# Mixing q and k per batch: z's high and low halves stacked on the partitions

## The reference

```python
W = weights[condition]                       # 64 x 64 for each batch
h = einsum('bct,bcd->bdt', x, W)             # mix the channels
qkv = einsum('bsc,cf->bsf', h, Wqkv) + bqkv  # 768 columns: q 256, k 256, v 256
attn = softmax(q @ k.T / sqrt(256))
x = x + (attn @ v) @ Wo + bo
```

## Time and profile before

| what | value |
|---|---|
| median of three runs | 2296.03 us |
| the profiled execution, its own time | 2296.87 us |
| its span (first to last instruction) | 2295.2 us |
| busy share of the span | PE 98%, weight loads 76%, DVE 54%, ACT 42% |
| granted TensorE clock, mean | 0.996 of full speed |
| chain that ended last | PE 95%, DMA 2%, DVE 1% |

### The profile page before, as it was taken

The page is one execution under the profiler, slowest core; times in us unless marked ns, Lnnn a source line. Parts: engine busy times, 40 slices in busy tenths (PEclk is TensorE's granted clock), DMA queues, the critical chain, the costliest instruction groups (busy, mean ns, idle before and its releaser), DMA issues.

```text
span 2295.2 us, 73807 instructions
## 1 busy us (share of the span) xinstructions
PE 2251.0 (98%) x28506; PEld 1753.5 (76%) x28506; DVE 1238.0 (54%) x3438; ACT 953.9 (42%) x2461; POOL 61.6 (3%) x128
## 2 busy tenths in 40 slices
PE   7999999999999879999999999999999999999998
PEld 4777777777777578887878787878787878787876
DVE  7777777777777753444344434443444344434443
ACT  5776777667776642222222222222222222222221
POOL 4000000000000000000000000000000000000000
PEclk9999999999999999999999999999999999999999
DMA  7668777677677742131123132113215132331303
GB/s 286 250 256 303 266 275 286 259 279 278 247 278 261 282 162 112 39 130 57 53 97 130 57 128 95 57 57 129 94 57 201 41 111 72 115 112 39 130 20 111
DMA packets 108960, 356.46 MB, mean 155 GB/s; under 512 B 27600, under 2 KB 28752, under 8 KB 79184
## 3 DMA queue, kind: packets, MB, share of 16 engines
q1 hardware_dynamic: 97584, 279.84, 33.7%
q0 software_dynamic: 10112, 72.36, 8.5%
q10 hardware_dynamic: 1056, 1.05, 0.1%
HBM read 218.99 MB, written 134.22 MB: 154 GB/s over the span
## 4 chain that ended last, share of the span: by engine, by line
PE 95%; DMA 2%; DVE 1%; issue 1%; SPq 0%; ACT 0%; POOL 0%; DVEq 0%; ACTq 0%; POOLq 0%
PE bank L1168 21%; PE bank L1299 19%; PE bank L1270 19%; PE bank L1272 10%; PE bank L1301 10%; PE bank L1125 4%; PE bank L1126 4%; PE bank L1127 4%; PE bank L1281 1%; PE bank L1308 1%; PE bank L1309 1%; DMA stage<-w_in 1%; PE bank L1283 1%; DMA x<-xr 1%; DVE wf L874 0%
## 5 line engine op out<-in xcount | busy, mean ns | idle before, releaser
L1270 PE MATMUL bank<-xs,w 128*128 128x128 f16 x8192 | 627.9, 220 | 9.4 <-DVE xs L881 9.4
L1168 PE MATMUL bank<-w,xs 128*128 128x384 f16 x3072 | 552.9, 327 | 4.4 <-DVE w L894 4.4
L1270 PEld LDWEIGHTS bank<-xs,w 128*128 128x128 f16 x8192 | 480.9, 98 | 11.3 <-issue 9.9
L1299 PE MATMUL bank<-y,wf 128*128 128x512 f16 x2048 | 483.8, 379 | 0.8 <-DVE xr L924 0.8
L763 ACT ACTIVATE zh<-bank 128x256 f32<-128x256 f32 x256 | 97.7, 382 | 779.7 <-PE bank L1272 776.9
L1168 PEld LDWEIGHTS bank<-w,xs 128*128 128x128 f16 x3072 | 290.5, 98 | 164.8 <-DVE w L894 2.6
L1272 PE MATMUL bank<-xs,w 128*128 128x64 f16 x8192 | 407.3, 193 | 0.0
L920 DVE SCALAR_TENSOR_TENSOR xr<-bank,xr 128x256 f32 (+1 forms) x256 | 108.8, 425 | 432.5 <-PE bank L1309 387.5
L1299 PEld LDWEIGHTS bank<-y,wf 128*128 128x128 f16 x2048 | 197.0, 98 | 186.5 <-DVE xr L924 1.1
L1272 PEld LDWEIGHTS bank<-xs,w 128*128 128x128 f16 x8192 | 337.3, 98 | 0.0
L1301 PE MATMUL bank<-y,wf 128*128 128x256 f16 x2048 | 265.3, 273 | 0.0
(11 more groups left out here) (158 smaller groups left out, 2087.1 us busy)
## 6 DMA issues: line engine op xcount, KB each, us to landing
stage<-w_in SPq DMA_DIRECT2D x68, 1024.0 KB, 8.9
w<-ws POOLq DMA_DIRECT2D x68, 1024.0 KB, 6.6
ws<-wf SPq DMA_DIRECT2D x64, 1024.0 KB, 6.9
out<-xr SPq DMA_DIRECT2D x128, 256.0 KB, 2.3
xr<-x_in SPq DMA_DIRECT2D x31, 1024.0 KB, 8.0
x<-xr SPq DMA_DIRECT2D x31, 1024.0 KB, 4.4
xr<-x SPq DMA_DIRECT2D x124, 256.0 KB, 3.5
wcf<-wc_in SPq DMA_DIRECT2D x128, 32.0 KB, 4.5
```

Source lines behind the costliest of these rows:

```text
L1168: e = mm(zps[q % 2][h][:, 0:384], lhs, rhs[:, k, h * 384:(h + 1) * 384], start=(k == 0 and lhs is a and rhs is wq_h), stop=(k == K - 1 and ...
L1270: mm(both, hi[:, k, c], x_k, start=(k == 0), stop=False)
L1299: mm(fps[m % 2][:, :], wf_h[:, k, c], yhl[:, u, k, :], start=(k == 0), stop=False)
```

## The change

The high and low half of one batch's z are stacked on the partitions of one tile, `zs`: for batch b, z's high half stays on that batch's 64 partitions and its low half is written on the other 64. The q and k columns of z now go into one PSUM bank (512 columns) and the v columns into another (256). The mixing matrix of each batch is loaded twice, on both halves of the partitions, so that one matmul with 128 rows sums high x matrix and low x matrix. A block is then two matmuls (`wch`, `wcl`) of 64 columns for each batch: 16 of 64 columns where there were 12 of 128. The v columns keep the old scheme in tiles of their own, `zvh` and `zvl`. `z_hi` and `z_lo` become three instructions each: two of 64 partitions x 512 columns and one of 128 x 256, each with its own signal.

```diff
+        zs = zs_flat[:, :].rearrange("p (r b n) -> p r b n", r=2, b=2)
+        zvh = sb("zvh", [P, 2, DH], F16)
+        zvl = sb("zvl", [P, 2, DH], F16)
...
+        ZCOLS = ((0, 2 * DH), (2 * DH, 3 * DH))
...
                     sp.dma_start(dst, src).then_inc(s_wc[n], 16)
+                    again = wcf[(1 - b) * S:(2 - b) * S, n, b * S:(b + 1) * S]
+                    sp.dma_start(again, wc_in[bass.ds(e, 1), :, 0, :].rearrange("a c d -> (a c) d")
+                                 ).then_inc(s_wc[n], 16)
...
             def z_hi(i, q):
                 wait(act, s_z, i, 4, q + 1)
-                for h in range(2):
-                    e = nc.scalar.activation(zh[:, q % 2, h * 384:(h + 1) * 384], zps[q % 2][h][:, 0:384], Copy,
-                                             scale=SZ / (SX * SW))
-                e.then_inc(s_zh, 1)
+                for b in range(2):
+                    at = slice(b * S, (b + 1) * S)
+                    nc.scalar.activation(zs[at, q % 2, b, :], zps[q % 2][0][at, :], Copy,
+                                         scale=SZ / (SX * SW)).then_inc(s_zh, 1)
+                nc.scalar.activation(zvh[:, q % 2, :], zps[q % 2][1][:, 0:DH], Copy,
+                                     scale=SZ / (SX * SW)).then_inc(s_zh, 1)
...
             def z_lo(i, q):
+                for b in range(2):
+                    wait(dve, s_zh, i, 12, 3 * q + b + 1)
+                    at, other = slice(b * S, (b + 1) * S), slice((1 - b) * S, (2 - b) * S)
+                    v.scalar_tensor_tensor(out=zs[other, q % 2, b, :], in0=zps[q % 2][0][at, :],
+                                           scalar=SZ / (SX * SW), in1=zs[at, q % 2, b, :], op0=ALU.mult,
+                                           op1=ALU.subtract).then_inc(s_zl, 1)
+                wait(dve, s_zh, i, 12, 3 * q + 3)
+                v.scalar_tensor_tensor(out=zvl[:, q % 2, :], in0=zps[q % 2][1][:, 0:DH],
...
-                        for h in range(2):
-                            e = mm(zps[q % 2][h][:, 0:384], lhs, rhs[:, k, h * 384:(h + 1) * 384],
+                        for h, (lo, hi) in enumerate(ZCOLS):
+                            e = mm(zps[q % 2][h][:, 0:hi - lo], lhs, rhs[:, k, lo:hi],
...
-                wait(pe, s_zl, i, 4, q + 1)
                 wait(pe, s_wcl, i, 4, q + 1)
-                for c in range(4):
-                    d = slice(c * P, (c + 1) * P)
-                    e = three(qkps[:, d], [(zh[:, r, d], zl[:, r, d], wch[:, r, 0:P], wcl[:, r, 0:P])])
+                for b in range(2):
+                    wait(pe, s_zl, i, 12, 3 * q + b + 1)
+                    at = slice(b * S, (b + 1) * S)
+                    for c in range(4):
+                        dst, z_c = qkps[:, c * P + b * S:c * P + (b + 1) * S], zs[:, r, b, c * P:(c + 1) * P]
+                        mm(dst, z_c, wch[:, r, at], start=True, stop=False)
+                        e = mm(dst, z_c, wcl[:, r, at], start=False, stop=True)
                 e.then_inc(s_qk, 1)
```

More of the change, by code:

```diff
@@ L113, in build @@
         xs = sb("xs", [P, 2, K, 2 * P], F16)
[L114 to L117, removed]
+        zs_flat = sb("zs", [P, 2 * 2 * 2 * DH], F16)
+        zs = zs_flat[:, :].rearrange("p (r b n) -> p r b n", r=2, b=2)
+        zvh = sb("zvh", [P, 2, DH], F16)
+        zvl = sb("zvl", [P, 2, DH], F16)
         qkh = sb("qkh", [P, 4, P], F16)
@@ L132, in build @@
         ol = sb("ol", [P, 2, 2, 2 * P], F16)
-        tt = zh_flat[:, 0:8 * P].bitcast(F32).rearrange("p (r m n) -> p r m n", r=2, m=2)
-        yf = zl_flat[:, 0:8 * P].bitcast(F32).rearrange("p (r m n) -> p r m n", r=2, m=2)
+        tt = zs_flat[:, 0:8 * P].bitcast(F32).rearrange("p (r m n) -> p r m n", r=2, m=2)
+        yf = zs_flat[:, 8 * P:16 * P].bitcast(F32).rearrange("p (r m n) -> p r m n", r=2, m=2)
         y_flat = sb("y", [P, 8 * K * P], F16)
@@ L638, in mix_hi @@
             def mix_hi(i, q):
-                wait(act, s_wc[q % 4], i, 32, 32 * (q // 4 + 1))
+                wait(act, s_wc[q % 4], i, 64, 64 * (q // 4 + 1))
                 wait(act, s_u, i, 4, q - 1)
@@ L927, in z_lo @@
             def z_lo(i, q):
-                wait(dve, s_zh, i, 4, q + 1)
-                for h in range(2):
[L930 to L934, removed]
+                for b in range(2):
[6 more added lines that the diff above has]
+                v.scalar_tensor_tensor(out=zvl[:, q % 2, :], in0=zps[q % 2][1][:, 0:DH],
+                                       scalar=SZ / (SX * SW), in1=zvh[:, q % 2, :], op0=ALU.mult,
+                                       op1=ALU.subtract).then_inc(s_zl, 1)
             def a_step(i, q, last=False):
@@ L1160, in z_part @@
                     wait(pe, s_xl, i, 4, q + 1)
-                    wait(pe, s_zl, i, 4, q - 1)
+                    wait(pe, s_zl, i, 12, 3 * (q - 1))
                 for k in ks:
@@ L1227, in a_step @@
                 wait(pe, s_ul, i, 4, q + 1)
+                wait(pe, s_zl, i, 12, 3 * q + 3)
                 for c in range(2):
-                    d = slice(2 * DH + c * P, 2 * DH + (c + 1) * P)
-                    e = three(chps[:, c * P:(c + 1) * P], [(zh[:, r, d], zl[:, r, d], uh[:, :], ul[:, :])])
+                    d = slice(c * P, (c + 1) * P)
+                    e = three(chps[:, d], [(zvh[:, r, d], zvl[:, r, d], uh[:, :], ul[:, :])])
                 e.then_inc(s_o, 1)
```

## The result

The changed kernel takes 2325.23 us (median of four runs, 2323.55 to 2327.47), beside 2296.07 us for the kernel before on the same chip: 1.0124 times as long, interval 1.0111 to 1.0136. It is slower by 29 us, where 13.5 us were forecast and the range ended at 2324. The profiled execution took 2325.25 us, with a span of 2323.6 us.

The account below looks back on a forecast made before the run. PE looked like the bound, with an almost equally long ACT and DVE path that would take over: 62 steps x 0.21 + 0.5 at the start = 13.5 us, giving 2309.5 us, 8-in-10 range 2301 to 2324.

Parts of the forecast that it names:

- Where the time goes: From z's end to the scores, the path over ACT and DVE sets the step: scores 0.21 us later each step.
- PE, q and k: Mixing of q and k on PE: 16 matmuls of 28.8 ns, 0.46 us instead of 0.67, saving 0.21 us.
- ACT, `z_hi`: Splitting z's high half on ACT: 1280 columns in three instructions instead of 768 in two, 0.49 us more a step.
- `z_hi` loses its overlap: Rival: ACT instructions on other partitions don't overlap, 2338 us, or 2322 us if two joins lose 0.1 each; chance 0.09.
- PE's slack: Before the score matmuls PE has no more than some 0.05 us to spare.
- DVE, `z_lo`: Splitting z's low half on DVE: 1280 columns in three instructions, no cost of its own, 0.14 us to spare.
- SP: Four more load issues in two steps, 2.6 us; the weight unit keeps 1.2 us of cover, so no cost.
- The start: At the kernel's start, extra issues stand between weight chunks: 0 to 1.5 us, taken as 0.5.

Follow-up runs that it names:

- `e1_split_only`: The kernel before with only the new three-instruction `z_hi` and `z_lo`; mixing and matrix loads as they were: 2324.55 us, 1.0119 times the kernel before.
- `e2_more_columns`: The kernel before with `z_hi` as 512, 512 and 256 columns, all on 128 partitions, the second 512 an unused copy: 2308.02 us, 1.0046 times.
- `e3_no_second_loads`: The changed kernel with each mixing matrix loaded on one half of the partitions only: 2324.09 us, 1.0122 times the kernel before.
- `e4_other_order`: The changed kernel with batch 1, on the upper partitions, taken before batch 0 in `z_hi`, `z_lo` and mixing: 2318.7 us, 1.0094 times the kernel before.
- `e5_pieces_moved`: The changed kernel with one weight-unit piece moved behind `qkh` and `qkl` and the third further down: 2301.84 us, 1.002 times the kernel before.
- `e7_order_and_pieces`: The changed kernel with batch 1 taken first and the weight-unit pieces moved later: 2301.17 us, 1.002 times the kernel before.
- `e9_loads_spread`: The changed kernel, batch 1 first, unit pieces later, one step's matrix loads before the x load, the next's behind the first unit's store and load: 2285.7 us, 0.9953 times.
- `e6_pieces_moved_before`: The kernel before with one weight-unit piece moved behind `qkh` and `qkl` and the third further down: 2295.27 us, 0.999 times the kernel before.

## Why the prediction was half right

*Where the time goes: right.* The path from z's end over `z_hi`, the unit pieces, `qkh` and `qkl` took PE's place. `qkl` releases the wait before the scores, `unit_lo` is released by the unit on ACT, and ACT's gap before `qkh` is gone. That the wait is listed with 0.46 us, where some 0.45 was forecast, is luck. The forecast was a distance of starts (414.23 against 413.8). By starts, the scores come 429.33 - 428.61 = 0.72 us after the output matmul ahead of them, where such matmuls had followed at 0.11: PE was held up for 0.61 us, the 0.20 that mixing had saved and the 0.41 that the step lost. The listed idle time is shorter, as the 0.27 us listed for the matmul ahead cover part of it.

*PE, q and k: right.* 0.47 us for 16 matmuls (0.46 forecast). The Trainium skill's 62 ns for each matmul with hardware decoding off ("TensorE: Matmul & The Clock Gate", section "Wait — 56ns, not 53.3ns?") would have made it 0.99; the trace has 29.4 ns and speaks against its holding here. The saving was hidden in the wait, as forecast: `e1_split_only` waits 0.21 us less.

**"ACT, `z_hi`" is the step that failed.** The term was 0.49 us, with bounds of 0.45 and 0.59, each of which took for granted that the three instructions overlap as their neighbours did. `e2_more_columns` shows that the columns are worth 0.48. But the new instructions begin at partition 0, 64 and 0, and the two changes cost 0.28 more: 0.76, outside the bounds. That was the milder case of the rival "`z_hi` loses its overlap", two joins of 0.1 each, with 2322 us and a chance of 0.09. By the prediction's own chain: 0.27 more on ACT, less the 0.05 of PE's slack that I left out of the likeliest case and `e2_more_columns` shows used up, makes 0.21 + 0.27 - 0.05 = 0.43 a step, and 0.42 was measured. The rival deserved more weight: no row of before had two neighbouring ACT instructions on different partitions, so nothing in the trace spoke for the overlap that the forecast assumed. And even the rival priced the two joins at 0.2 us, where they cost 0.28.

*DVE, `z_lo`: no cost, right, though the joins that the sum counted on were lost.* Two instructions of 0.689 us span 1.41, and the third waits for their end. That each `z_lo` now has a wait of its own isn't the reason: in `e2_more_columns` each has one too, and its two, of 0.692 and 0.415 us on all partitions, span 1.02 us and so overlap. So the Trainium skill's rule in "VectorE: DVE Perf Modes", section "Two Vector instructions with no wait between them", that an instruction beginning in another group of 32 partitions is held until those before it are done, agrees with this trace. The loss didn't set the time, since ACT's delay was larger: DVE still idles 0.17 us before `unit_lo`. For DVE the prediction priced the lost joins; for ACT, with the same change of partitions, it kept them out of its bounds and left them to a rival. ACT loses them too, by the runs.

*SP: no cost in the steady state, right* (`e3_no_second_loads`), but with little to spare, and in another place than the prediction looked. It followed the weight unit; what came late was the matrices themselves. Two steps of 12.9 us wait for one, and when the step became shorter, that wait returned as the next bound (`e4_other_order`, `e5_pieces_moved`, `e7_order_and_pieces`). *The start* was given 0.5 us for the extra issues and lost 1.7, but no run shows those issues to cost that much: `e1_split_only` has none of them and starts its fourth `z_hi` at 61.2 us, `e9_loads_spread` has them all and starts it at 59.3. The clock makes most of the difference.

In part open: what the weights that POOL loads do to the matrices. In `e7_order_and_pieces` POOL issues such loads at 107.7, 205.6, 304.5 and 403.3 us, and the four long steps start at 107, 205, 304 and 403. In `e4_other_order` and `e5_pieces_moved` such a load is issued in each long step too, and so it is in the two steps of 12.9 us of the changed kernel. In `e9_loads_spread` the four loads are issued as well, from 107.5 to 392.6 us, and no step there takes more than 12.5 us. So the long steps come where POOL's load meets the old order on SP with the second loads in it; a run without POOL's loads was not made.

## What to carry to other kernels

When an edit splits one instruction over ranges of partitions, add the lost overlap at each change of the first partition to the columns; if no row shows such a neighbour, the bounds must hold the case without overlap. A saving on the engine that is 100% busy is worth nothing while another path ends at the same moment: take work off that path in the same edit, and then look at what the shorter step makes late, here the transfers and their order on one queue.

## What the runs showed of the hardware that was not expected

- On ACT, an instruction of 512 columns from PSUM takes 592 to 594 ns on 64 or 128 partitions alike; its neighbour starts 0.49 us after it if it begins at the same partition (1.08 - 0.594) and 0.62 us after it if not (1.21 - 0.592). That the first partition matters, and not their number, is shown by `e4_other_order`, where 128 partitions from 0 overlap with 64 from 0. Source and destination of these instructions changed their first partition together in every run; which of the two counts is not shown.
- TensorE's clock fell to 0.50 after waits of 2.84 us (changed kernel) and 2.30 us (`e7_order_and_pieces`), and stayed at 1.00 after one of 2.85 us (`e3_no_second_loads`). After 2.28 us it stayed at 1.00 in the kernel before and fell in `e6_pieces_moved_before`.
- In one queue, what was issued ahead of what decided between 2285.7 and 2321.99 us for the same transfers and the same compute.
